# Causal masks in an attention: each GpSimd selection on the 64 partitions of its half, and the inverse roots two steps earlier

## The reference

```python
x = x + state_space_convolution(layernorm(x))
x = x + experts(layernorm(x))          # 8 experts, top 2 weighted
x = x + attention(layernorm(x))
x = x + experts(layernorm(x))          # the same weights again
```

```python
att = einsum('bhqd,bhkd->bhqk', q, k) * scale
att = where(causal, att, -inf); att = softmax(att, axis=-1)
y = einsum('bhqk,bhkd->bhqd', att, v)
```

## Time and profile before

| | |
|---|---|
| time, median of 3 runs | 786.8 us (785.27 to 787.71) |
| time of the profiled execution | 785.32 us |
| its span | 783.6 us |
| TensorE busy | 730.7 us (93%) |
| VectorE busy | 678.6 us (87%) |
| ScalarE busy | 671.6 us (86%) |
| GpSimd busy | 564.3 us (72%) |
| GpSimd's selections, L1323 | 384 in 311.3 us |

### The profile page before, as it was taken

One profiled execution on the slowest core, in us unless ns is written; L12 is line 12 of the kernel. 1 busy time (PEld: TensorE's weight loads), 2 busy tenths in 40 slices (PEclk: granted clock), 3 DMA queues, 4 the chain that ended last, 5 costly groups with the idle time before them and its releaser, 6 DMA issues.

```text
span 783.6 us, 21138 instructions
## 1 busy us (share of the span) xinstructions
PE 730.7 (93%) x8042; PEld 410.2 (52%) x8042; DVE 678.6 (87%) x1958; ACT 671.6 (86%) x932; POOL 564.3 (72%) x622
## 2 busy tenths in 40 slices
PE   4798999999999899999999999999889999999996
PEld 3345667777776333333333333333325777677774
DVE  7998999899887878889989998878787889989885
ACT  5918999999998988888888888888976999899984
POOL 2898676665445999999999999999974445445542
PEclk9999999999999999999999999999999999999998
DMA  9210000000044244343444533554300000000000
GB/s 279 58 80 28 2 2 2 2 2 2 2 109 101 65 111 99 102 103 82 102 109 102 107 92 95 108 97 94 67 3 1 15 1 15 15 15 15 15 15 18
DMA packets 37964, 45.74 MB, mean 58 GB/s; under 512 B 6137, under 2 KB 23810, under 8 KB 37858
## 3 DMA queue, kind: packets, MB, share of 16 engines
q1 hardware_dynamic: 37858, 44.33, 23.0%
HBM read 27.53 MB, written 16.78 MB: 57 GB/s over the span
## 4 chain that ended last, share of the span: by engine, by line
PE 64%; DVE 18%; ACT 10%; issue 5%; POOL 2%; DMA 0%; ACTq 0%; DVEq 0%; POOLq 0%
PE psum L1379 15%; PE psum L1028 15%; PE psum L959 14%; PE psum L1307 7%; ACT prob L1314 6%; DVE mixed L1047 4%; PE psum L1447 4%; PE psum L1182 3%; ACT hidden_first L973 1%; ACT hidden_parts_first L975 1%; PE psum L698 1%; PE psum L1249 1%; DVE normed L394 1%; DVE stats L374 1%; DVE o_tok L1389 1%
## 5 line engine op out<-in xcount | busy, mean ns | idle before, releaser
L1314 ACT ACTIVATE prob<-psum 128x1280 f32<-128x1280 f32 x256 | 299.2, 1241 | 46.5 <-PE psum L1307 46.5
L1323 POOL TENSOR_SCALAR_AFFINE_SELECT prob<-prob 128x768 f32<-128x768 f32 (+1 forms) x384 | 311.3, 847 | 22.2 <-ACT prob L1314 20.6
L959 PE MATMUL psum<-xt_parts,w_parts 128*128 128x512 f16 x768 | 186.6, 379 | 0.0
L1379 PE MATMUL psum<-prob,vstack 128*32 128x512 f32 (+1 forms) x1536 | 167.0, 533 | 5.1 <-DVE o_tok L1389 2.2
L989 POOL TENSOR_TENSOR hidden_parts_second<-hidden_second,hidden_parts_second 128x512 f16<-128x512 f32 x64 | 77.6, 1213 | 94.8 <-ACT hidden_parts_second L975 94.8
L1047 DVE SCALAR_TENSOR_TENSOR mixed<-psum,comb_y,mixed 128x128 f32<-128x128 f32 x512 | 143.2, 340 | 1.6 <-PE psum L1028 1.5
L989 POOL TENSOR_TENSOR hidden_parts_first<-hidden_first,hidden_parts_first 128x512 f16<-128x512 f32 x64 | 79.2, 1238 | 73.0 <-ACT hidden_parts_first L975 73.0
L1307 PE MATMUL psum<-qstack,kstack 32*64 32x512 f16 (+1 forms) x1536 | 100.0, 362 | 14.8 <-ACT prob L1314 13.3
L959 PEld LDWEIGHTS psum<-xt_parts,w_parts 128*128 128x128 f16 x768 | 70.9, 98 | 65.0 <-issue 1.4
L973 ACT ACTIVATE hidden_second<-psum,b 128x512 f32<-128x512 f32 x128 | 88.4, 691 | 16.4 <-PE psum L959 14.9
L1028 PEld LDWEIGHTS psum<-w_parts,hidden_parts_first 128*128 128x128 f16 x1536 | 90.3, 98 | 19.6 <-issue 6.7
(11 more groups left out here) (155 smaller groups left out, 880.3 us busy)
## 6 DMA issues: line engine op xcount, KB each, us to landing
qstack<-qk_parts SPq DMA_DIRECT2D x128, 128.0 KB, 3.5
qk_parts<-parts SPq DMA_DIRECT2D x64, 192.0 KB, 3.2
kstack<-qk_parts SPq DMA_DIRECT2D x128, 32.0 KB, 3.5
stream<-u_folded SPq DMA_DIRECT2D x4, 512.0 KB, 7.8
kept_x<-stream SPq DMA_DIRECT2D x4, 512.0 KB, 2.7
out<-mixed SPq DMA_DIRECT2D x7, 256.0 KB, 2.3
w_whole<-L_ffn_W SPq DMA_DIRECT2D x1, 1024.0 KB, 9.0
taps<-c_taps SPq DMA_DIRECT2D x1, 640.0 KB, 6.9
```

What stands on the lines that cost most here:

```text
L959: last = e.matmul(bank(u % 4), m.w1[:, w_part, ex, cols], xt_parts[:, s, x_part, :], start=(n == 0), stop=(n == len(PRODUCTS) - 1))
L1314: e.activation(prob[:, n % PROBS, 0:COLS], psum[:, TILE * (n % 2):TILE * (n % 2) + COLS], ACT.Exp, scale=SCALE)\
L1323: return e.affine_select(kept, kept, [[0, n] for n in kept.shape[1:-1]] + [[sign, BLK]], ALU.is_ge, 0.0, base=BLK * half, channel_multipli ...
L1379: last = e.matmul(to[SLOT * lane:SLOT * (lane + 1)], vstack[:, b % 2, kind, c * LANES + lane].rearrange("p h r -> p (h r)"), weights_of(q, ...
```

## The change

Each selection is put on the 64 partitions that it changes, and the two of a mask follow each other directly, both after the exponential of their step; the waits of the second on the first go with the semaphore half_masked. masked counts both selections, so the waits for it are doubled. The 13 inverse roots go from the ninth to the seventh step of their batch, a step without a mask; ahead of them GpSimd waits until the selections of steps 4 and 5 have ended, and between the two selections of the eighth step it waits until the root has. In the first step of all, it waits between the two for its own last subtraction of the first experts.

```diff
-    def gpsimd_masked(e, kept, half):
-        sign = 1 if half else -1
-        return e.affine_select(kept, kept, [[0, n] for n in kept.shape[1:-1]] + [[sign, BLK]], ALU.is_ge, 0.0,
-                               base=BLK * half, channel_multiplier=-sign)
-    def gpsimd_second_half_mask(e, m):
-        q, t = divmod(m, MASKS_Q)
-        e.wait_ge(exped, 4 * q + t + 1 + t // 2)
-        gpsimd_masked(e, mask_place(m), 0).then_inc(half_masked, 1)
-
-    def gpsimd_first_half_mask(e, m):
-        e.wait_ge(half_masked, m + 1)
-        gpsimd_masked(e, mask_place(m), 1).then_inc(masked, 1)
+    def mask_place(m, rows):
...
+            return prob[rows, slot].rearrange("p (n l g q) -> p n l g q", n=3, l=2, q=BLK)[:, :, 0]
+        return prob[rows, slot:slot + 2, 2 * BANK:COLS].rearrange("p n (g q) -> p n g q", q=BLK)
+
+    def gpsimd_half_mask(e, m, half):
+        kept, sign = mask_place(m, slice(BLK * half, BLK * (half + 1))), 1 if half else -1
+        e.affine_select(kept, kept, [[0, n] for n in kept.shape[1:-1]] + [[sign, BLK]], ALU.is_ge, 0.0, base=0,
+                        channel_multiplier=-sign).then_inc(masked, 1)
+
+    def root_of(b):
+        if b % 2 == 0 and b // 2 + 2 < FFN_CHUNKS:
+            return mixed_norm, b // 2 + 2
+        if b % 2 and b >= 3:
+            return expert_norm, second.at + (b - 3) // 2
 
     def gpsimd_mask(e, n):
         q, t = divmod(n, 4)
-        m = MASKS_Q * q
-        if t == 0:
-            gpsimd_second_half_mask(e, m)
-            if q:
-                gpsimd_first_half_mask(e, m - 1)
-        elif t == 1:
-            gpsimd_second_half_mask(e, m + 1)
-            gpsimd_first_half_mask(e, m)
-            gpsimd_first_half_mask(e, m + 1)
-        elif t == 3:
-            gpsimd_second_half_mask(e, m + 2)
+        if t != 2:
+            e.wait_ge(exped, n + 1)
+            gpsimd_half_mask(e, MASKS_Q * q + t - t // 2, 0)
+            if n == 0:
+                e.wait_ge(low_second, EXPERTS * FFN_CHUNKS)
+            elif n % STEPS_B == 7 and (root := root_of(n // STEPS_B)):
+                e.wait_ge(root[0].rstd, root[1] + 1)
+            gpsimd_half_mask(e, MASKS_Q * q + t - t // 2, 1)
...
         elif kind == EARLY:
-            e.wait_ge(masked, MASKS_Q * q + 2)
+            e.wait_ge(masked, HALVES * (MASKS_Q * q + 2))
         else:
-            e.wait_ge(masked, MASKS_Q * (q + 1))
+            e.wait_ge(masked, HALVES * MASKS_Q * (q + 1))
...
     def gpsimd_attention(e):
         for n in range(LAST):
             b, at = STARTS[n]
-            if at == 8 and b % 2 == 0 and b // 2 + 2 < FFN_CHUNKS:
+            if at == 6 and root_of(b):
+                e.wait_ge(masked, HALVES * MASKS_Q * (n // 4) + HALVES * 2)
+            if at == 6 and b % 2 == 0 and b // 2 + 2 < FFN_CHUNKS:
                 gpsimd_mixed_rstd(e, b // 2 + 2)
-            if at == 8 and b % 2 and b >= 3:
+            if at == 6 and b % 2 and b >= 3:
                 gpsimd_route_rstd(e, second, (b - 3) // 2)
             gpsimd_mask(e, n)
-        gpsimd_first_half_mask(e, MASKS_Q * QUADS * BATCH - 1)
+        e.wait_ge(masked, HALVES * MASKS_Q * QUADS * BATCH)
```

More of the change, by code:

```diff
@@ L341, in build_in @@
     s_stack = [sem(f"stack_landed{i}") for i in range(2)]
-    scored, exped, half_masked, masked, weighed = (sem(n) for n in (
-        "scored", "exped", "second_half_masked", "masked", "weighed"))
+    scored, exped, masked, weighed = (sem(n) for n in (
+        "scored", "exped", "masked", "weighed"))
     turned, inverted_den, o_normed, rows_up, in_count, projected, attn_done = (sem(n) for n in (
@@ L1315, in scalar_exp @@
          .then_inc(exped, 1)
-    def gpsimd_masked(e, kept, half):
-        sign = 1 if half else -1
-        return e.affine_select(kept, kept, [[0, n] for n in kept.shape[1:-1]] + [[sign, BLK]], ALU.is_ge, 0.0,
-                               base=BLK * half, channel_multiplier=-sign)
-    def mask_place(m):
+    def mask_place(m, rows):
         q, t = divmod(m, MASKS_Q)
@@ L1329, in mask_place @@
         if t < 2:
-            return prob[:, slot].rearrange("p (n l g q) -> p n l g q", n=3, l=2, q=BLK)[:, :, 0]
-        return prob[:, slot:slot + 2, 2 * BANK:COLS].rearrange("p n (g q) -> p n g q", q=BLK)
-    def gpsimd_second_half_mask(e, m):
-        q, t = divmod(m, MASKS_Q)
-        e.wait_ge(exped, 4 * q + t + 1 + t // 2)
-        gpsimd_masked(e, mask_place(m), 0).then_inc(half_masked, 1)
-    def gpsimd_first_half_mask(e, m):
-        e.wait_ge(half_masked, m + 1)
-        gpsimd_masked(e, mask_place(m), 1).then_inc(masked, 1)
+            return prob[rows, slot].rearrange("p (n l g q) -> p n l g q", n=3, l=2, q=BLK)[:, :, 0]
[9 more added lines that the diff above has]
+            return expert_norm, second.at + (b - 3) // 2
     def gpsimd_mask(e, n):
         q, t = divmod(n, 4)
-        m = MASKS_Q * q
-        if t == 0:
-            gpsimd_second_half_mask(e, m)
-            if q:
-                gpsimd_first_half_mask(e, m - 1)
-        elif t == 1:
-            gpsimd_second_half_mask(e, m + 1)
-            gpsimd_first_half_mask(e, m)
-            gpsimd_first_half_mask(e, m + 1)
-        elif t == 3:
-            gpsimd_second_half_mask(e, m + 2)
+        if t != 2:
[6 more added lines that the diff above has]
+            gpsimd_half_mask(e, MASKS_Q * q + t - t // 2, 1)
     def weights_of(q, kind, lane):
```

## The result

The changed kernel takes 803.92 us in the median of 4 runs (802.29 to 804.63), against 786.51 us for the kernel before (785.27 to 787.71): 1.023 of it, 95% interval 1.0209 to 1.025. It is 17.4 us slower, where 2.9 us less was forecast. The range ended at 786.8; slower had a chance of 0.07.

A forecast was written before the change was run, and what follows sets the result against it. The prediction took TensorE and ScalarE to bound the steady batches, with GpSimd's saving hidden. Gains elsewhere of 1.2 + 1.35 + 0.3 = 2.9 us took the median from 786.8 to 783.9 us, range 781.8 to 786.8.

The forecast's parts named there:

- The slower rival: Attention batches: GpSimd becomes the pace if serial selections are over 47 ns dearer each; at 75 ns +11 us, 798; chance 0.06.
- Steady batches nothing: Regular attention batches: no gain, as the chain is TensorE and ScalarE and GpSimd's saving is hidden under TensorE's 20.56 us.
- (a): Batches 5, 9 and 13, where a range check makes VectorE late: 3 x 0.41 = 1.2 us gained, bounds 0 and 1.2.
- (b): Last batch: earlier inverse root and less blocking of VectorE start the last quad's sums 1.35 us earlier; bounds 0.6 and 1.35.
- (c): Between 564 and 573 us, VectorE on the chain: 0.3 us gained with TensorE's second stall; bounds 0 and 0.4.

## Why the prediction was wrong

**The step that failed** is the choice of a bound: "the halves are worked on by different parts of GpSimd, and two of them together take what one takes", taken at 6 or 7 in 10. Both halves of that are wrong. They don't run side by side, and a selection on 64 partitions isn't even as cheap as one on 128 behind another: it costs 0.107 us more, because it starts on other partitions than the one ahead. The two memsets of the earlier trace rows, 50 ns apart, were the evidence. But by the kernel's code both start on partition 0 (128 partitions, then 0 to 63), so they show nothing of two halves, and short memsets overlap on all 128 partitions too. Two of four at the start of the trace before (timeline):

```profile
0.32 0.10 POOL L2242 MEMSET const-float32-0.0<- 128x1 f32 x1 [0.32 <-issue]
0.35 0.10 POOL L2242 MEMSET const-float32-1.0<- 128x1 f32 x1
```

The row of a subtraction on 32 partitions, 1145 against 1210 ns, was the better one.

The Trainium skill (GPSIMD Engine Reference, 2.1 Instruction dispatch) has each core serve its own 16 partitions and go on by itself. The trace doesn't agree for neighbours on different halves: the second starts 65 ns after the end of the first, not beside it.

**The slower rival had the mechanism, and a price too low.** "Serial selections dearer by over 1.12 / 24 = 47 ns each make it the bound of every batch": they are dearer by 107 ns, and in the changed kernel's steady batches it is. Its sum at 75 ns was 28 x 384 ns = 11 us. In the same way 107 ns give (107 - 47) x 384 = 23 us; 17.4 were measured. Three terms are off. The slack is not 1.12 but 2 x 0.47 = 0.94 us a batch of waits for exponentials; the rest are two gaps of 0.11 and 0.07 us between selections. This alone would make the loss larger. But GpSimd's own time rose by 22.60 - (21.34 - 0.94) = 2.20 us a batch, where 24 x 0.107 = 2.57: 0.37 us came back. That VectorE's product is blocked less (502 against 802 ns) suggests that the two collide less; that this is where the 0.37 us come from was not tried. The batch period grows by 22.60 - 21.34 = 1.26 us. Over 15 batches that would be 18.9 us and is 17.7: the first three and the last three lose less each, while the pairs with batch 5 and 9 lose more, 3.0 us (43.09 to 46.10) and not 2.5. The last batch gives 2.0 us back, most of it by the clock, and the last stall takes 1.3.

The premise stood: "a batch period other than 21.34 us, which would mean that GpSimd or the blocked VectorE does hold the steady chain" was named as the sign of wrong, and it is what came. What deserved weight was GpSimd's 20.22 of 21.34 us: the forecast gave 0.06 to a case that needed only 47 ns on a 913 ns instruction whose new form no row showed.

**The parts behind the failed step, tested alone.** Steady batches nothing: right, 21.33 us at half the selections. (a) 3 x 0.41 us: nearly right with half the load, 0.43 + 0.43 + 0.16 = 1.03 us; the third pair had only 0.16 to give, and the chain of the trace before shows only two such pairs. Not reached in the change. (b) 1.35 us: with half the load and the root in its old place the last sums start 1.87 us earlier, of which 1.03 are (a), so some 0.8 us are (b) and (c) together, where 1.65 were forecast. TensorE's clock was lower in that trace's last batch (0.86 against 0.93), which may hide a part. With the root moved alone 0.46 us is seen there (591.85 - 591.39), close to the lower bound of 0.6 that the forecast named; the 1.4 us less of the whole run is measured to about 1.1 us either way. (c), the stall of the earlier trace rows at 573: 1.57 us with the root moved, 1.25 with half the load, against 1.58: 0.3 us, as taken. The sum of 2.9 us against 2.7 measured looks exact and is partly luck: the interval reaches from 1.7 to 3.8, the traces show 1.7 to 1.9, and the run lacks the earlier root that the sum counts in. The direction and the rough size were right, for work that the change didn't do.

**Waits.** "Neither costs anything" was said of the removed waits and the doubled counts. Right: the old order hid its waits, as none was on the selection directly ahead. So removing them could gain nothing. A wait on the one directly ahead would have cost 0.11 us, the price of a change of half; the new order pays that price at every selection, six times a quad.

**Open.** Whether a change costs because the starts differ or because no partition is shared. Why three changes a quad (793.6 us) cost 3.4 us more than three waits (790.2), which add as much to GpSimd by themselves: L384 is held longer (mean 930 against 740 ns), but no run isolates it. How the loss of two and three changes splits between GpSimd's time and the held L384, which is read from the batches that have it short or long and from the chain, and whether moving L384 wins it back. And whether an order of 64-partition selections exists that is placed beside VectorE's work so as to lose nothing.

## What to carry to other kernels

An engine whose waits are short and whose work is 95% of the period is one small surcharge away from being the bound: divide its slack by its instructions (here 0.94 us / 24 = 39 ns) and ask of every new form of instruction whether it could cost that. Narrowing an instruction's partitions saved nothing on GpSimd in any row here, and alternating between two starts is a cost; keep neighbours in the queue on the same start, and put a selection that waits for another at least one instruction behind it. Look also at the small instructions of an engine that GpSimd can hold up: one of 0.17 us on the chain became 0.92 and the batch longer by 0.3 us. When the price of a new form decides the sign, no neighbouring row replaces it: eight of them in a row in a program of their own gave it in one run.

## What the runs showed of the hardware

- GpSimd, one selection of 768 elements: 0.858 us from start to start on 32, 64, 96, 112 and 128 partitions alike; one takes 0.90 us, so the next starts some 45 ns before its end.
- A change of the first partition between neighbours: +0.10 to 0.11 us, for selections of 256 and 768 elements, additions, scalings and memsets, between any two starts tried (0 and 32, 0 and 64, 0 and 96; the two never shared a partition). The next starts some 65 ns after the end of the one ahead. A narrower instruction with the same first partition: nothing.
- A wait on the instruction directly ahead: the same 0.11 us; on an earlier one: not measurable (0.86 us from start to start).
- VectorE's sum of 4 elements a partition (L384): 0.17 us, or up to 0.93 beside GpSimd's selections, and then it ends 22 to 28 ns after one of GpSimd's instructions.
